# Transformer block with routed experts: the second round of expert tiles walked in three levels, six of eight output chunks finished inside the tile loop

## What is computed

```python
probs = softmax(logits); tk_probs, tk_idx = top_k(probs, 2)      # tk_probs normalised
out = _swiglu(xf, sWg, sWu, sWd)                                  # shared expert, all rows
for e in range(NUM_EXPERTS):                                      # 8 experts, HIDDEN 128, INTER 256
    out = out + w[:, e:e + 1] * _swiglu(xf, Wg[e], Wu[e], Wd[e])
x = x + _layernorm(out)                                           # x: 4 x 1024 rows of 128
```

## Time and profile before

| what | us |
|---|---|
| time, median of 3 runs | 835.36 |
| lowest and highest run | 835.12, 839.98 |
| the profiled execution's own time | 839.22 |
| its span (first to last instruction) | 837.5 |
| TensorE busy in the span | 753.9 |

### The profile page before, as it was taken

One profiled execution on the slowest core, in us unless ns is written; L12 is line 12 of the kernel. 1 busy time (PEld: TensorE's weight loads), 2 busy tenths in 40 slices (PEclk: granted clock), 3 DMA queues, 4 the chain that ended last, 5 costly groups with the idle time before them and its releaser, 6 DMA issues.

```text
span 837.5 us, 17519 instructions
## 1 busy us (share of the span) xinstructions
PE 753.9 (90%) x5660; PEld 361.6 (43%) x5660; DVE 620.7 (74%) x1942; ACT 510.1 (61%) x1047; POOL 338.3 (40%) x517
## 2 busy tenths in 40 slices
PE   5876689999999999999999999999989889898994
PEld 2332133333334334334333433433336768786861
DVE  5998878988887896886897887888445566465636
ACT  2664046666766877766778666687887534343525
POOL 3775121222221331234543215453257276464624
PEclk9997579999999999999999999999999999999998
DMA  6459462431632423405324224141312325232153
GB/s 161 149 156 178 119 166 31 67 52 17 116 57 44 79 46 73 80 8 110 59 61 94 53 39 86 40 98 40 118 37 71 104 79 146 72 85 71 50 205 112
DMA packets 78187, 71.84 MB, mean 86 GB/s; under 512 B 26939, under 2 KB 58076, under 8 KB 77916
## 3 DMA queue, kind: packets, MB, share of 16 engines
q1 hardware_dynamic: 69472, 59.87, 32.4%
q0 software_dynamic: 4352, 8.99, 3.4%
q10 hardware_dynamic: 4274, 1.87, 0.9%
HBM read 44.27 MB, written 23.94 MB: 81 GB/s over the span
## 4 chain that ended last, share of the span: by engine, by line
PE 62%; DVE 11%; issue 7%; ACT 6%; POOL 1%; DMA 1%; POOLq 0%; SPq 0%; DVEq 0%; ACTq 0%
PE ps L2171 14%; PE ps L2198 14%; PE ps L305 11%; DVE x_in L316 5%; PE ps L1668 4%; ACT expT L1895 4%; PE ps L1649 2%; PE ps L1651 2%; PE ps L1657 2%; PE ps L1650 2%; PE ps L1573 1%; PE ps L2148 1%; PE ps L1586 1%; ACT rows L747 1%; PE ps L972 1%
## 5 line engine op out<-in xcount | busy, mean ns | idle before, releaser
L1895 ACT ACTIVATE expT<-ps 128x512 f32<-128x512 f32 (+1 forms) x640 | 333.0, 554 | 149.6 <-PE ps L2198 143.4
L316 DVE CUSTOM_DVE_ANT_0 x_in<-ps,mask 128x1024 bf16<-128x1024 f32 (+7 forms) x512 | 364.3, 754 | 60.5 <-PE ps L305 57.0
L2198 PE MATMUL ps<-q_space,k_space 96*128 96x512 bf16 (+3 forms) x768 | 223.6, 334 | 8.8 <-ACT expT L1895 5.1
L305 PE MATMUL ps<-k_space,q_space 96*128 96x512 bf16 (+3 forms) x768 | 197.6, 343 | 22.1 <-DVE mx L316 15.5
L2171 PE MATMUL ps<-expT,vr 128*9 128x256 f32 (+1 forms) x2560 | 178.3, 360 | 0.9 <-POOL expT L1849 0.9
L1849 POOL TENSOR_SCALAR_AFFINE_SELECT expT<-expT 128x512 f32<-128x512 f32 x128 | 79.7, 634 | 195.9 <-ACT expT L1895 195.5
L2198 PEld LDWEIGHTS ps<-q_space,k_space 96*128 96x128 bf16 x768 | 62.1, 98 | 160.3 <-ACT expT L1895 103.1
L305 PEld LDWEIGHTS ps<-k_space,q_space 96*128 96x128 bf16 x768 | 64.1, 100 | 86.2 <-DVE mx L316 49.0
L1255 POOL DMA_INDIRECT expert_rows<-expT,tile_to x72 | 69.2, 961 | 49.8 <-ACT expT L1326 24.1
L737 POOL DMA_INDIRECT sorted_rows<-rows,places x64 | 64.2, 1003 | 58.2 <-ACT expT L1895 33.9
L2171 PEld LDWEIGHTS ps<-expT,vr 128*9 128x9 f32 x2560 | 41.3, 88 | 92.2 <-issue 47.1
(11 more groups left out here) (228 smaller groups left out, 934.1 us busy)
## 6 DMA issues: line engine op xcount, KB each, us to landing
q_space<-q_parts SPq DMA_DIRECT2D x48, 192.0 KB
expT<-sorted_rows SPq DMA_DIRECT2D x72, 65.0 KB, 2.1
k_space<-k_parts SPq DMA_DIRECT2D x32, 128.0 KB
expT<-expert_rows SPq DMA_DIRECT2D x16, 256.0 KB, 5.4
q_parts<-parts SPq DMA_DIRECT2D x24, 128.0 KB, 2.4
k_parts<-parts SPq DMA_DIRECT2D x24, 128.0 KB, 3.2
k_space<-k_parts SPq DMA_DIRECT2D x16, 192.0 KB
v_ones<-v_st SPq DMA_DIRECT2D x8, 288.0 KB, 3.2
```

The costliest lines, as they stand in the source:

```text
L305: last = nc.tensor.matmul(psw[:, at + lo:at + hi], qr[:, g % RING, hh, qi * P:(qi + 1) * P], kr[:, g % RING, hh, lo:hi], start=True, stop= ...
L316: last = nc.vector.tensor_tensor_reduce(out=unread[:, odd, col:col + width], in0=psw[:, 2 * CT * odd + col:2 * CT * odd + col + width], in ...
L1895: act.activation(expT[:, (NS * g + s) % PTN, hh, 0:width], ps[:, B_S + hh % 2, 0:width], ACT.Exp, scale=SCALE).then_inc(exp_ok, 1)
L2198: last = nc.tensor.matmul(ps[:, B_S + hh % 2, col:col + m], kr[:, g % RING, hh, kt * P:(kt + 1) * P], qr[:, g % RING, hh, q0:q0 + m], star ...
```

## The change

1. **Three levels.** The second round of tiles no longer goes expert by expert over all rows. It walks three levels: what is left of pairs 0 and 1 for all experts, then pair 2, then pair 3. The bounds in the code are `LEVEL1_PAIRS` = 20 and `LEVEL2_PAIRS` = 28: behind step 19 all rows of chunks 0 to 3 are done, behind step 27 those of chunks 4 and 5. The number of steps stays 36.
2. **The table on 128 partitions.** Partition k computes tile k. The tables work on 8 or 24 numbers in each partition, the division by 128 is a multiplication and a rounding, and SyncE copies the two columns to rows with small transfers (`tiles_to_row`). `late_table` has eight parts, two in each of the steps 0 to 3.
3. **Six chunks finished among the tiles.** Chunks 0 to 5 no longer go through `sum_rows`. VectorE adds the two picks to the shared part in SBUF (`join_y`, two additions of 128x512). The work of chunks 0 to 3 stands in a table by step, between `tile_h` and `keep_lo`: a and b are `join_y`, s is `out_stats`, j `out_join`, h `out_shift`, r `out_row`. GpSimd's `out_root` of chunks 0 to 3 stands behind the scatters of steps 26, 29, 32 and 35. ScalarE's `out_norm` of chunks 0 to 2 stands at the end of steps 27, 30 and 33, that of chunk 3 between the silus of chunk 6. Chunks 4 and 5 are joined behind the last step, among the `gated` of chunks 6 and 7. SyncE reads chunks 0 to 3 within steps 28 to 31 of its own order.

```diff
+            PIECES = {23: ["a0"], 24: ["b0"], 25: ["s0"], 26: ["j0", "a1"], 27: ["h0", "b1"], 28: ["s1"], 29: ["j1", "r0"],
+                      30: ["h1", "a2"], 31: ["b2"], 32: ["s2", "j2"], 33: ["r1", "h2", "a3"], 34: ["b3", "s3"], 35: ["j3", "r2"]}
+            ROOT_AT, NORM_AT = (26, 29, 32, 35), (27, 30, 33)
...
@@ SyncE
                 for q in range(EARLY_TILES // 2, NP):
                     if 2 * q % BATCH == 0:
                         sp.load(regs, row_at[0:1, 2 * q:2 * q + BATCH])
                     rows_of_tiles(q)
-
-                for r in range(TILE_RING):
-                    sp.wait_ge(y_sent[r], y_sent_until(r, NP - TILE_RING + r))
-                for c in range(CHUNKS):
-                    for k in range(2):
-                        get_y(sp, c, k)
-                for c in range(CHUNKS):
+                    if 0 <= q - TILE_RING - LEVEL1_PAIRS + 1 < IN_TILES:
+                        both(q - TILE_RING - LEVEL1_PAIRS + 1)
+                for q in range(NP - TILE_RING, LEVEL2_PAIRS):
+                    rows_done(q)
+                for c in range(IN_TILES, IN_TILES + IN_GAP):
+                    both(c)
+                for c in range(IN_TILES - 1):
+                    store_out(sp, c)
+                for q in range(LEVEL2_PAIRS, NP):
+                    rows_done(q)
+                for c in range(IN_TILES + IN_GAP, CHUNKS):
+                    both(c)
+                for c in range(IN_TILES - 1, CHUNKS):
                     store_out(sp, c)
@@ GpSimd, in the loop over q, behind the two scatters
-                for c in range(CHUNKS):
+                    if q in ROOT_AT:
+                        out_root(ROOT_AT.index(q))
+                for c in range(IN_TILES, CHUNKS):
                     out_root(c)
@@ ScalarE
                     if q > 0:
                         keep_y(q - 1)
+                    if q in NORM_AT:
+                        out_norm(NORM_AT.index(q))
                 silu(FRONT, 0)
                 keep_y(NP - 1)
                 silu(FRONT, 1)
+                out_norm(3)
                 silu(FRONT + 1, 0)
                 silu(FRONT + 1, 1)
@@ VectorE
+                def join_y(c, k):
+                    dve.wait_ge(y_got[c], 2 * DMA)
+                    if k == 0:
+                        dve.wait_ge(sh_kept, c + 1)
+                    else:
+                        dve.wait_ge(y_joined, 2 * c + 1)
+                    v.tensor_tensor(shared(c), shared(c), y_in(c)[:, k], ALU.add).then_inc(y_joined, 1)
...
                     tile_h(q)
-                    if 1 <= q <= LATE_PARTS:
-                        late_table(q - 1)
+                    if 2 * q < LATE_PARTS:
+                        late_table(2 * q)
+                        late_table(2 * q + 1)
+                    for piece in PIECES.get(q, ()):
+                        finish(piece)
                     if q + 2 < NP:
                         keep_lo(q + 2)
                     else:
                         lo(dve, FRONT + q + 2 - NP)
                 keep_hT(NP - 1)
-                for c in range(FRONT, CHUNKS):
-                    gated(c, 0)
-                    gated(c, 1)
+                out_shift(3)
+                join_y(4, 0)
+                gated(FRONT, 0)
+                join_y(4, 1)
+                gated(FRONT, 1)
+                out_stats(4)
+                out_join(4)
+                gated(FRONT + 1, 0)
+                out_row(3)
+                gated(FRONT + 1, 1)
+                join_y(5, 0)
+                join_y(5, 1)
+                out_shift(4)
+                out_stats(5)
...
@@ TensorE
-                for c in range(CHUNKS):
+                for c in range(FRONT, CHUNKS):
                     sum_rows(c)
```

More of the change, by code:

```diff
@@ L1306, in scalar_behind, with out_norm @@
                 keep_shared(5)
+                def out_norm(c):
+                    wait(act, yo_ok, c - 1)
+                    act.wait_ge(shift2_ok, c + 1)
+                    for t in range(NT):
+                        last = act.activation(yn[:, c % 2, t], summed(c)[:, t], ACT.Identity, scale=rstd2[:, c, t:t + 1],
+                                              bias=nb2[:, c, t:t + 1])
+                    last.then_inc(normed2, 1)
                 def keep_hi(q):
@@ new lines, in late_table @@
+                        dve.wait_ge(table2, 4)
+                        v.tensor_tensor(seg_n[:].rearrange("p l e -> p (l e)"), ends[:], first[:, 0:n], ALU.subtract).then_inc(table2, 1)
+                        v.tensor_tensor(seg_rows[:], first[:, 1:n + 1], ends[:], ALU.subtract).then_inc(table2, 1)
+                    elif part == 2:
+                        dve.wait_ge(table2, 5)
+                        for l in range(LEVELS):
+                            last = v.tensor_tensor(tri2[:, l], upto_of, seg_n[:, l].unsqueeze(1).to_broadcast([P, NE, NE]), ALU.mult)
+                        last.then_inc(table2, 1)
@@ L1503, in keep_hT, with out_row, finish @@
                     v.tensor_copy(hT[:, q % 2], ps[:, B_HT]).then_inc(hT_ok, 1)
+                def out_row(c):
+                    dve.wait_ge(normed2, c + 1)
+                    dve.wait_ge(mid_back, DMA * (CHUNKS - 2))
+                    wait(dve, y_out[c % 2], DMA * (c // 2))
+                    v.tensor_tensor(yo[:, c % 2], yn[:, c % 2], x_mid(c), ALU.add).then_inc(yo_ok, 1)
+                def finish(piece):
+                    kind, c = piece[0], int(piece[1])
+                    if kind in "ab":
+                        join_y(c, "ab".index(kind))
+                    elif kind == "s":
+                        out_stats(c)
+                    elif kind == "j":
+                        out_join(c)
+                    elif kind == "h":
+                        out_shift(c)
+                    else:
+                        out_row(c)
                 keep_lo(0)
@@ L1518, in vector_behind @@
                 keep_hT(NP - 1)
[L1519 to L1539 removed]
+                out_shift(3)
[12 more added lines that the diff above has]
+                out_stats(5)
+                out_join(5)
+                out_row(4)
+                out_shift(5)
+                out_stats(6)
+                out_join(6)
+                out_row(5)
+                out_stats(7)
+                out_shift(6)
+                out_join(7)
+                out_row(6)
+                out_shift(7)
+                out_row(7)
             def tensor_behind(pe, item):
```

278 lines of the change are left out of this document (141 added, 137 removed).

## The result

The changed kernel takes **852.6 us** (median of 4, 852.12 to 854.33) against 835.64 for the kernel before in the same job: ratio 1.0195, 95% interval [1.0163, 1.0226]. It is slower by 1.6 to 2.3%. The profiled execution took 854.33 with a span of 852.6; the one of before 839.22 with 837.5, so the two traces differ by 15.1.

A forecast was written before the change was run, and what follows sets the result against it. TensorE, busy in 90% of the span, was taken to bound the kernel. Terms 16.2 + 3.1 + 1.2 - 9.8 + 3.9 = +14.6 us, set against the 835.36 median, gave 850, range 842 to 858.

The forecast's parts named there:

- Three stalls, +16.2: Steps 27, 30, 33: VectorE's out_shift waits for GpSimd's root behind scatters, 5.4 us each, +16.2 us.
- The other pieces, +3.1: Loop steps 25 to 35: VectorE's additions, out_stats and out_join beyond the free 0.6 us a step, +3.1 us (1 to 5).
- The table, +1.2: Steps 0 to 3: two table parts each, some 0.2 us per small instruction, +1.2 us (0 to 2).
- The end, -9.8: From the last tile_down to the last out_row: 25.2 us instead of 35.0, -9.8 us (-6 to -12).
- with no wait at `out_shift(3)` it would be some 4 more: Ending: if VectorE did not wait for chunk 3's root, the end would gain some 4 us more.
- The clock, +3.9, three falls at 1.3: TensorE's granted clock falls behind the four waits, three falls at 1.3 us, +3.9 us (0 to 6.8).
- my upper bound: Upper end of the clock term, for falls behind TensorE's four waits: 6.8 us.
- One of the signs that I named: New profile's loop: tile_down groups 8.5 us apart at the three out_shift waits and 3.2 elsewhere.
- The roots are in time: Rival: GpSimd has each root done when VectorE asks, no stalls, -9.5 us, 826; chance 0.07.
- The stalls are there, the clock holds: Rival: loop and end waits occur but TensorE's clock does not fall, +10.7 us, 846; chance 0.2.
- Half a stall: Rival: VectorE's standing costs TensorE only 3 us each time and the clock holds, +3.5 us, 839; chance 0.06.
- The reads are late as well: Rival: join_y(0, 0) in step 23 waits for reads, VectorE stands 2 us more; 855 with four clock falls; chance 0.12.

The follow-up runs named there:

- moved_free: Changed kernel with powers ahead of scatters, out_shift/out_norm one step later, first y addition in step 24, and gated, silu(7) ahead of out_shift(3), out_norm(3): 826.76 us, ratio 0.9868.
- levels_alone: Changed kernel's three levels and table, with the end of the kernel before (eight sum_rows, no chunk finished in the loop): 837.8 us, ratio 0.9998.
- tail_free: Changed kernel; behind the last tile, VectorE's gated(6) and joins come ahead of out_shift(3), ScalarE's silu(7) ahead of out_norm(3): 847.51 us, ratio 1.0104.
- filled: Changed kernel with 38 unused matmuls of 256 columns ahead of tile_down in steps 28, 31 and 34, filling TensorE's idle time: 848.47 us, ratio 1.0123.
- waits_alone: Kernel before plus only three waits: GpSimd powers behind scatters of steps 26, 29, 32, awaited by VectorE in steps 27, 30, 33: 856.0 us, ratio 1.0198.
- moved_tail: Changed kernel with powers ahead of scatters, out_shift/out_norm one step later, first y addition in step 24, and gated(6), join_y(4) ahead of out_shift(3): 828.33 us, ratio 0.9883.
- roots_first: Changed kernel with each of the first four roots ahead of its step's two scatters on GpSimd instead of behind them: 833.37 us, ratio 0.9937.
- shift_tail: Changed kernel with out_shift and out_norm of chunks 0 to 2 two steps later, and gated, silu(7) ahead of out_shift(3), out_norm(3): 830.36 us, ratio 0.9891.

## Why the prediction was right, point by point

The time of 852.6 lies 2.6 above the forecast of 850.0 and in its range of 842 to 858, and the mechanism is the one named. Set against the sum, term by term:

- **Three stalls, +16.2.** Measured 5.07 + 4.95 + 5.37 = 15.4. The order of events was as counted from the earlier trace rows. One link was too large: the power takes 1.04 in the loop, not the 1.31 of the earlier trace rows or the 1.4 that I took. The 1.31 was a mean over powers at the end of the kernel.
- **The other pieces, +3.1.** In the changed kernel little of it shows (+0.35 at step 25, 0.2 in all at 29 and 32), since most pieces fall into steps that are late anyway. In `moved_free`, where no step is late, the steps from 24 to 35 take 38.26 instead of 34.42 us: +3.8. With the 0.2 to 0.4 us in each step behind a stall it is 1.4. The term was about right for a loop without stalls, and counted some 1.7 us too much in this one.
- **The table, +1.2.** In the changed kernel `tile_h` is 1.78 us earlier than before at step 0 and 1.22 at step 5, so the table costs 0.6; `levels_alone` shows the same (0.5). Within the bounds given (0 to 2), and twice what it came to. The estimate of 0.2 us for one small instruction of the table had no row behind it; in the changed kernel 20 of these 22 take 0.15 to 0.22.
- **The end, -9.8.** Measured -8.1 from the last `tile_down`, -8.5 from `tile_h(35)`. I had put "with no wait at `out_shift(3)` it would be some 4 more"; it is 5.5 more (29.65 against 24.12 in `tail_free`). The term is short by the clock behind that wait (0.50 from 828 to 834): `down(6)` takes 3.4 us instead of the 1.8 that I counted, and the sum has the clock only in its last term.
- **The clock, +3.9, three falls at 1.3.** This is the term that was mis-sized. All four waits brought a fall (the granted clock is 0.50 from 777 to 783, 794 to 800, 811 to 817 and 828 to 834), and each fall of the loop cost 2.3 to 2.5 us by `filled`, 7.3 together (6.0 in the whole time). With 1.6 at `down(6)` and 1.3 at step 24 (below) it is some 10 us against 3.9. No run shows the term of 3.9, nor 1.3 as the price of a fall behind a wait of 5 us; the runs showed the 2.3 to 2.5 in its place. I had looked at the falls behind waits of 1.42 and 1.54 us. In windows of 1 us the clock stands at 0.50 for some 3.4 us behind each of them; half of that, 1.7 us, is an estimate of what one costs, and four of them are the 6.8 of my upper bound. Behind a wait of 5 us, in which TensorE does 3.18 us of work in 8, the slow stretch was twice as long, some 6.8 us, and the upper bound for all four was still below the loop's 7.3 alone.

The terms that erred low (clock) and high (pieces, table, the stalls by 0.8) nearly cancel. So does something that no term has: in the two traces the changed kernel is 1.8 us earlier at `tile_h(0)` and 0.9 us shorter at step 11, where `tile_h(0)` lies between 672.3 and 678.4 in all kernels and step 11 takes 7.0 to 8.4. These 2.6 us differ from execution to execution. The mechanism was right; that the time came within 3 us is in part luck. One of the signs that I named was off: I had `tile_down` 8.5 us apart at a stall and 3.2 elsewhere, and it was 8.0 there and 5.7 right behind.

**The rivals.** *The roots are in time* fell: none was. *The stalls are there, the clock holds* fell in the changed kernel, and `filled` shows what it would have been in the loop: 1.0123 times 835.64 is 845.9, where I had said 846. *Half a stall* fell: 5.1 us a time, not 3. *The reads are late as well* was true in part, and its price was not where I had put it. VectorE waits in step 23 for the first rows of y, only 0.54 us, but the step is 2.26 longer than before. `tile_down(23)` starts 3.26 us behind `tile_h(23)` instead of 2.27, which is 1.0 for the wait and the addition:

```profile
751.78 0.69 DVE L1424 TENSOR_TENSOR q_space<-q_space,expT 128x512 f32<-128x512 f32 x1 [0.54 <-DMA expT<-expert_rows]
```

```profile
753.81 1.15 PE L1764 MATMUL ps<-w_gu,k_space 128*128 x8 [1.86 <-DVE k_space L1574]
756.34 0.79 PE L1745 MATMUL ps<-w_hi,rows_hi 128*128 x1 [1.37 <-issue]
```

Before:

```profile
755.04 1.15 PE L1668 MATMUL ps<-w_gu,k_space 128*128 x8 [0.87 <-DVE k_space L1503]
```

The other 1.3 is the clock, which falls behind the register load of step 24: the granted clock is 0.50 from 757 to 759, and a matmul that takes 0.48 us at 1.00 takes 0.79 here. In the seven kernels whose first addition stands in step 23, the changed one among them, `tile_h(24)` comes 8.92 to 9.38 us after `tile_h(23)`; in the three where it stands in step 24 it is 8.13, 7.11 and 7.07, and before 7.12. A fall at this place needs no late read: `waits_alone`, which has no such addition, has one and took 8.04, and the 8.13 is another. So the clock fell here, to 0.50 in windows of 1 us between 756 and 765, in all seven kernels with the addition in step 23, and in two of the six others; in the kernel before, `levels_alone`, `moved_tail` and `moved_free` it is 1.00 in all of them. That the addition there makes a fall likelier is what these counts say, one trace of each kernel; why was not tried by itself.

**Where the expected gain of the change went.** The shorter end is real: 8.5 us as it stands and 13.5 in `moved_free`. It was paid for with three waits in a loop where VectorE feeds TensorE in every step, with a fourth behind it, and with a slow clock after each (0.50 for some 6.8 us).

## What to carry to other kernels

Before a small result of another engine is waited for inside a tight loop, look at what stands ahead of it in that engine's queue: here VectorE stood 5.2 us for a power of 1.04 us, because two scatters stood before it and the first of them waited for ScalarE, and moving it in front of them was worth 2.6%. In this loop a wait of some 5 us on TensorE's path cost 40 to 50% more through the clock (2.3 to 2.5 us by `filled`), so a stall has to be priced with the step behind it. Work taken off the end and put among the tiles paid most (0.9868) where each piece found its inputs ready; with waits of 1.6 us it still paid (0.9937), with waits of 5 it cost more than it brought.

## What the runs showed of the hardware that I had not expected

- The same power (128x4) takes 1.007 to 1.046 us in all eight places of the changed kernel, and 1.31 on average before. Before, two of the eight take 1.01 and 1.04 and six take 1.39 to 1.42, and each of those six starts while an `out_row` of VectorE has 0.52 to 0.56 us to go. In the changed kernel an `out_row` lies wholly inside two of the powers, which take 1.007; and one power of `moved_tail` takes 1.60 with only 0.10 us of an `out_row` at its start. Whether the overlap at the start is the cause was not tried.
- The slow stretch behind a 5 us stall of the changed kernel, some 6.8 us at a granted clock of 0.50, cost 2.3 to 2.5 us. With matmuls in the stall there was none (1.00 from 770 to 820 in `filled`), and behind a wait of VectorE of 1.58 us (`roots_first`) there was no fall (1.00 from 772 to 824).
- Matmuls without use, 38 of 256 columns three times, made the changed kernel 0.7% faster.
- The ratios of one kernel's runs spread by up to 1% (826.7 to 834.62 for `shift_tail`), and the profiled executions differ by up to 6 us already at `tile_h(0)`, with the clock falling at step 12 in some and not in others (`tile_h(12)` 7.04 to 8.35 us after `tile_h(11)`; the granted clock is 0.50 in windows of 1 us between 714 and 720 in eight of the thirteen traces, and 1.00 from 706 to 722 in the other five).
